# A two-layer gated cross-attention and expert stack: the fourth score wave of the first attention's loop moves from ahead of the fifth pair to ahead of the sixth

## The reference, cut to what matters

```python
x = x + tanh(g_xattn[0]) * L0_xattn(layernorm(x), ctx)     # the change lies here
x = x + tanh(g_ffn[0])   * L0_ffn(layernorm(x))            # top-1 of 8 experts
x = x + tanh(g_xattn[1]) * L1_xattn(layernorm(x), ctx)     # ternary weights, int8 activations
x = x + tanh(g_ffn[1])   * L1_ffn(layernorm(x))            # gated mixture of 16 projections

# L0_xattn: B=8 batches, N=100 tokens, M=361 context rows, 16 heads of 16
q = (x @ Wq + bq).reshape(B, N, 16, 16)
k = (y @ Wk + bk).reshape(B, M, 16, 16)
v = (y @ Wv + bv).reshape(B, M, 16, 16)
scores = einsum('bnhd,bmhd->bhnm', q, k) / 4
out = einsum('bhnm,bmhd->bnhd', softmax(scores), v)
h = relu(out @ W1 + b1) @ W2 + b2
```

## Time and profile before

| | us |
|---|---|
| median of 3 runs | 597.01 (595.83 to 597.95) |
| the profiled execution | 595.76, of which the span is 593.6 |
| PE busy | 578.7 (97%) |
| DVE busy | 385.5 (65%) |
| ACT busy | 219.2 (37%) |
| passes 0 to 6, wave 0 of pass 0 to the maxima's transposes behind pass 6 | 58.9 to 165.1 of the span |

### The profile page before, as it was taken

How to read it: one execution, slowest core, us unless ns; L and a number is a source line. 1 busy time by engine, 2 the same in 40 slices (tenths; PEclk the granted TensorE clock), 3 DMA queues, 4 the chain that set the end, 5 groups by cost and what they waited for, 6 DMA issues and landing times.

```text
span 593.6 us, 10354 instructions
## 1 busy us (share of the span) xinstructions
PE 578.7 (97%) x3971; PEld 428.8 (72%) x3971; DVE 385.5 (65%) x928; ACT 219.2 (37%) x513; POOL 137.3 (23%) x172
## 2 busy tenths in 40 slices
PE   9999999999999999999999989999999999999997
PEld 7766344544456767999999748767787888887587
DVE  1996767587884765222222579886999879775454
ACT  3554665566673374222222376585200010001000
POOL 0053200114004402222222000004355555440000
PEclk9999999999999999999999999999999999999999
DMA  8920000002001562999998100610733662320001
GB/s 187 314 106 1 19 1 1 14 26 57 2 1 28 202 216 79 314 334 368 330 328 294 64 2 0 208 43 1 255 128 105 210 219 89 107 81 0 1 28 29
DMA packets 25695, 71.07 MB, mean 120 GB/s; under 512 B 5271, under 2 KB 13063, under 8 KB 21815
## 3 DMA queue, kind: packets, MB, share of 16 engines
q1 hardware_dynamic: 21910, 58.15, 30.1%
q0 software_dynamic: 3744, 12.38, 6.3%
HBM read 65.02 MB, written 5.49 MB: 119 GB/s over the span
## 4 chain that ended last, share of the span: by engine, by line
PE 76%; DVE 17%; ACT 3%; DMA 2%; issue 1%; SPq 0%; POOL 0%; DVEq 0%; POOLq 0%
PE bank L2193 10%; PE bank L1999 8%; PE bank L2012 8%; PE bank L1821 8%; PE bank L2271 7%; PE bank L1666 7%; PE bank L2181 6%; PE bank L1795 5%; PE bank L1839 3%; PE bank L1764 2%; PE bank L1827 2%; DMA x<-in_x 2%; DVE stats L586 1%; PE bank L1645 1%; DVE nmax L1063 1%
## 5 line engine op out<-in xcount | busy, mean ns | idle before, releaser
L2193 PEld LDWEIGHTS bank<-region,kvT 128*128 128x128 f32 x448 | 77.0, 190 | 9.9 <-issue 0.9
L2193 PE MATMUL bank<-region,kvT 128*128 128x200 f32 x448 | 81.1, 333 | 0.8 <-DVE region L1180 0.8
L761 DVE TENSOR_REDUCE nmax<-bank 100x2 f32<-100x722 f32 x64 | 55.2, 905 | 24.8 <-PE bank L1795 24.4
L1999 PEld LDWEIGHTS bank<-stage,region 128*128 128x128 f32 x448 | 52.1, 192 | 1.4 <-issue 0.8
L1999 PE MATMUL bank<-stage,region 128*128 128x128 f32 x448 | 52.4, 275 | 0.5 <-ACT stage L1490 0.5
L2012 PE MATMUL bank<-region,stage 128*128 128x256 f32 x224 | 50.7, 379 | 0.0
L2181 PE MATMUL bank<-region,kvT 128*128 128x400 f32 x128 | 48.5, 502 | 0.6 <-DVE region L1187 0.6
L2012 PEld LDWEIGHTS bank<-region,stage 128*128 128x128 f32 x224 | 41.5, 190 | 5.1
L2271 PE MATMUL bank<-region,kvt 128*128 128x200 f32 (+1 forms) x192 | 44.5, 389 | 0.3 <-DVE region L1247 0.3
L977 DVE TENSOR_SCALAR stage<-bank,stage 128x128 f32<-128x128 f32 x56 | 15.8, 344 | 44.2 <-PE bank L1999 44.2
L1513 ACT ACTIVATE stage<-bank,stage 128x128 f32<-128x128 f32 x56 | 16.0, 368 | 66.3 <-PE bank L1999 46.6
(11 more groups left out here) (360 smaller groups left out, 1094.9 us busy)
## 6 DMA issues: line engine op xcount, KB each, us to landing
region<-in_e_w SPq DMA_DIRECT2D x28, 1024.0 KB, 4.9
kvT<-in_p_qkv SPq DMA_DIRECT2D x32, 384.0 KB, 3.1
stage<-w_dram POOLq DMA_DIRECT2D x2, 1600.0 KB, 13.6
stage<-in_t_f SPq DMA_DIRECT2D x1, 2048.0 KB, 15.0
kvt<-in_p_o SPq DMA_DIRECT2D x1, 2048.0 KB, 8.7
stage<-in_e_b SPq DMA_DIRECT2D x14, 128.0 KB, 6.1
region<-in_ctxT SPq DMA_DIRECT2D x3, 541.5 KB, 14.0
stage<-w_dram POOLq DMA_DIRECT2D x3, 400.0 KB, 5.3
```

What stands on the lines that cost most here:

```text
L761: dve.tensor_reduce(nmax[:, b % 2, at_h:at_h + 9:8], banks[0:N, bank:bank + 2, 0:M], AX.X, ALU.max, negate=True)\
L1999: ins = pe.matmul(psum[2 * u + m // 4][:, (m % 4) * P:(m % 4 + 1) * P], e_w1[u][:, k, m * P:(m + 1) * P], xsT[u][:, k, :], start=k == 0, s ...
L2193: return pe.matmul(bank, left, right, start=e == 0 and i % 2 == 0, stop=e == E1 - 1 and i in (1, 3, 5, 6))
```

## The change

Wave 3 of batch n+1 is issued at u = 10, ahead of the values and of the sixth pair, in place of u = 8, ahead of the fifth pair. So PE runs the fourth and the fifth pair, with their chain units, one behind the other. Nothing is added, removed or resized, and the programs of DVE, ACT, POOL and SP are the same.

```diff
                     if u == 4 and n == B:
                         first_product(0, 1)
+                    if u == 10 and n + 1 < B:
+                        score_wave(n + 1, 3)
                     if u in (6, 10) and 1 <= n <= B:
                         values(n - 1, u // 2 - 3)
                         values(n - 1, u // 2 - 2)
-                    if u in (6, 8) and n + 1 < B:
-                        score_wave(n + 1, u // 2 - 1)
+                    if u == 6 and n + 1 < B:
+                        score_wave(n + 1, 2)
                     if n < B and u % 2 == 0:
                         score_pair(n, u)
```

## The result

The changed kernel takes 602.94 us (median of 6, 601.66 to 610.46), the kernel before beside it 597.08 (median of 6). The ratio is 1.0121, interval 1.0089 to 1.0154: slower, as forecast, but by 5.9 us at the medians and not by 2.3, and outside the range that ended at 601.2. The profiled execution took 601.80 with a span of 599.7, against 595.76 and 593.6.

A forecast was written before the change was run, and what follows sets the result against it. PE, busy 97% of the span at full clock, was taken as the bound. Terms 1.36 + 3 x 0.21 - 2 x 0.19 + 0.71 = +2.32 us on a base of 596.64 gave 599.0 us, range 597.0 to 601.2.

The forecast's parts named there:

- The wait that goes: Wave 3's second half no longer waits for DVE: 0.42 saved in passes 1, 2, 6; 0.83 in 3, 4.
- Two pairs in a row, 0.63 and 0.64: Fifth pair waits for ACT to empty shared banks: costs 0.63 with chain units, 0.64 in pass 3 without.
- rival 2: The fifth pair finds its banks free and does not wait for ACT: -2.2 us, 594.4; chance 0.07.
- Pass 5, +0.71: No lateness to save; fifth pair's second product waits for a chain unit's bank, freed by ACT's accumulator read: +0.71 us.
- Pass 0's late transposes, +1.36: No values cover the late maxima in pass 0, so transposes start at 74.78 in place of 73.42: +1.36 us.
- Rival 3: Pass 0's late transposes paid only in part, or the shift given back behind the loop: +1.0, 597.6; chance 0.16.
- Pass 6, hidden by ACT: Pass 6's transposes would be late, but ACT holds the pair behind them until 166.28 after the change: hidden.
- the transposes can start 4.40 after wave 3 does: Earliest start of the transposes: DVE needs 4.34 from wave 3's start to the split's end, a semaphore 0.06 more.
- its masking waits for pairs that stay ahead: POOL's masking of the queries waits for pairs a whole pass ahead of where its result is needed; no cost counted.
- Rival 1: DVE falls behind in passes 1, 2 and 5 too, each missing by 0.3 to 0.5: +2.9 to +3.9, 600 us; chance 0.14.
- The margins that it went by, 0.25 and 0 us: Time by which the values still hide the late transposes: 0.25 us in passes 1 and 5, 0 in pass 2.
- Rival 4: PE's clock falls behind pass 0's new gap of 1.36 us: +4 to +17 us; chance 0.03.

The follow-up runs named there:

- with the mask late: The changed kernel with POOL's masking of the queries waiting one unit more, for the maxima's transposes: median 601.3 us, ratio 1.0085 to the kernel before.

## Why the prediction was wrong

- **The wait that goes.** Right. Wave 3 takes 0.80 in all passes of the changed kernel; in pass 3 a total unit runs in between and the values start 0.98 after the wave.
- **Two pairs in a row, 0.63 and 0.64.** Right: 2.08 between the chain units in passes 0, 1 and 6, so rival 2 is out, and with the mask late the passes that carry these terms alone (1 to 5) came within 0.12 us of the forecast each.
- **Pass 5, +0.71.** Right: +0.70 with the mask late. In the changed kernel it shows as +0.42, since its first pair was held by ACT before, a hold that the late transposes now cover.
- **Pass 0's late transposes, +1.36.** Right in mechanism: 1.43 with the mask late. In the changed kernel 1.80, since the cast (line 771) took 0.56. Rival 3, that it is paid only in part, is out by the run with pass 0 in the order of before (2.0 us back).
- **Pass 6, hidden by ACT.** Right. From the transposes to pass 7's first chain unit it is 1.31 us now and was 1.96:

```profile
171.12 0.34 PE L1808 MATMUL bank<-ident_bf,small 100*128 100x100 bf16 x4 [0.56 <-DVE small L774]
...
172.43 0.48 PE L1764 MATMUL bank<-stage,tern 128*128 128x361 bf16 x2
```

- **The step that failed** is "the transposes can start 4.40 after wave 3 does", used for each pass as if the durations in it did not depend on where they fall, and, for POOL, the sentence that its masking waits for pairs that stay ahead. That looked at who feeds POOL and who waits for it, and not at what runs on DVE at that moment. A cast or subtraction that takes 0.2 us was held for up to 1.48 by POOL's 1.52 us mask, and in passes 1 to 4 the split took 1.1 to 1.3 us longer. The spans of the two profiled executions differ by 6.1 us, 3.8 more than the forecast; the missing term is 3.2 of these (6.24 less 3.07 by the passes). About 0.1 more lies in the passes, and the other 0.5 outside them (0.3 earlier at their start, 0.8 later behind them); no run was made for that part. Without the missing term the loop comes out at +2.4, against the +2.32 of the sum.
- **Rival 1** had part of the outward form (transposes late in passes 1 and 2, which the prediction itself had named as a sign of being wrong; those of pass 5 were not late) but too small a loss, +2.9 to +3.9, and another cause, and its "its durations repeat within 0.01" was true only of a kernel in which the two never met. The margins that it went by, 0.25 and 0 us, were real and small, and passes 3 and 4, which were held to be safe, were hit as well.
- **Rival 4**, the clock, was given 0.03. Four of the first six runs had a mean clock under 0.998, and with them the median of 602.9 lies 1.2 us over the two at full clock. That these falls come from the new gap is not shown, and the traced run, 601.8 at full clock, is already outside the range by the missing term alone.

The kernel before did show the hold, from the other side. The mask takes 1.52 us in passes 0 to 3. Here, ahead of pass 0 and at the end of pass 4, it met longer DVE instructions:

```profile
57.60 2.35 DVE L726 SCALAR_TENSOR_TENSOR tern<-region,wabs,tern 128x2048 bf16<-128x2048 f32 x1
...
58.55 2.78 POOL L488 TENSOR_TENSOR w_a<-xn,consts 128x800 f32<-128x800 f32 x1 [9.69 <-PE bank L1666]
...
132.38 0.54 DVE L673 TENSOR_SCALAR stage<-region 128x722 bf16<-128x722 f32 x1
...
132.46 1.83 POOL L488 TENSOR_TENSOR xT<-xn,consts 128x800 f32<-128x800 f32 x1 [12.84 <-PE bank L1827]
```

There it was POOL that was held: 2.78 and 1.83 us, each ending 1.4 us behind DVE's instruction. One instruction with the same shape and three durations is the row that should have been asked about. The Trainium skill, page "SBUF — State Buffer", section "Who interferes with whom", says it as a rule: DVE and GpSimd share a pair of ports; a DVE copy, cast or `tensor_scalar` may need it, and so does an instruction with both inputs in SBUF when the GpSimd one reads SBUF; whichever comes first holds the other off for its whole length, while a reduction never contends. The traces agree in each point that they touch: casts and subtractions held for up to 1.48 us, the reductions of lines 747 and 761 not at all.

## What to carry to other kernels

When a step is moved, ask of each instruction whose time shifts by it not only who feeds it and who waits for it, but also what runs beside it on DVE and POOL; a 0.2 us instruction can cost the length of the longest one of the other engine. A stretch of margin on a helper engine (here 0.25 us) is no cover until the instruction that it is made of is known to keep its length. To take a wait away, put independent work of the waiting engine ahead of it (the third group of values, with the mask out of the way: -0.4%) rather than work that draws on another scarce buffer.

## What the runs showed of the hardware

- A DVE cast or subtraction of 100 by 16 elements, 0.2 us alone, lasted 1.33 to 1.48 us when it started early in a POOL instruction of 1.52 us (0.56 when it met the end of one), and at most 0.82 beside halves of it. DVE's reductions kept their 0.52 and 0.90 us beside the same instruction.
- With a gap of 1.7 us on TensorE, the mean granted clock was under 0.998 in 10 of 10 runs; with idle products in the gap in 4 of 10, without the gap in 9 of 33. In the one trace with the gap the clock was full for 74 us before it and fell to half behind it. The runs with the gap took 599.1 to 601.8 us against 596.8 of the kernel before at full clock, of which the gap itself is 1.8.
- In all kept traces together, TensorE's waits of 1.44, 1.45, 1.72 and 2.34 us were each followed by a stretch at 1.2 GHz, and some twenty waits of 0.9 to 1.3 us by none. Two more falls, at 420 and 427 us, came behind pairs of shorter waits (0.67 and 0.76; 0.45 and 0.75 us), while the changed kernel's trace has 0.46 and 0.76 in the same place and kept its clock.
